# A graph network kernel: layer 1's two norms, residual and next product in one chunked pass, and a bias as a 65th row of weights

## The chip, the core and the metric

The kernel runs on one core of a Trainium2 chip. The core has a matrix engine (TensorE, PE in the profile; PEld are its weight loads), a vector engine (VectorE, DVE), an activation engine (ScalarE, ACT), GpSimd (POOL), which here mostly issues gathers and scatters by index, and SyncE (SP), which issues the other transfers. The metric is device microseconds of one launch, lower is better.

## What is computed

Four residual graph layers on 6250 nodes of 128 features and 106250 edges. Each is fed by `h = relu(layernorm(x))`. The stretch that is changed lies between the first layer's result and the third layer's first product:

```
h = relu(layernorm(x));  x = x + L0(h)            # two attention layers, then a dense product with Wlin, blin
h = relu(layernorm(x));  x = x + L1(h)            # L1: xw = h @ W; out = adjacency-weighted sum of xw, + b;
                                                  #     out = layernorm(out) * ln_gamma + ln_beta
h = relu(layernorm(x));  x = x + L2(h)            # L2 begins with h[src] @ W1.T + b1, taken here as (h @ W1.T + b1)[src]
```

## The kernel before, in words

The nodes lie as 49 blocks (`NB`) of 128 rows, one row to a partition, so a tensor of all nodes is 128 partitions x 6272 elements. `Xn` holds x, `B0`, `B1`, `B2` are buffers of that size, `accn` is another in `ACC`. Work "by chunk" takes four blocks (`CB`), so 13 chunks (`CHUNKS`), the last with one block. A stage ends with a barrier of all engines (`end`, `S.end_stage`). The stages around the change, in order:

- `into_layer_1` (L2126): a software pipeline by chunk, its order written out in `on_vector`, `on_scalar`, `on_tensor` (at step s, chunk s minus a fixed lag). DVE mixes (`mix`, L2174 and L2180), ACT takes exp and relu, DVE joins them (L2196), PE turns the chunk (`turn`, L2203), ACT copies it (L2210), PE multiplies it by Wlin (`multiply`, 64 rows of weights, L2218) and adds the bias with a second matmul of one row of ones (L2219), ACT takes exp and relu of the result (L2227, L2228), DVE adds it to x with row sums (`join_again`, L2236, L2241, L2244), ACT in `norm` makes relu(x - mean) (L2252) and the squares (L2256), PE turns it again (L2263) and multiplies by the layer's W (`multiply_again`, L2276), and DVE moves it to `B1` (`move`, L2282). After all chunks DVE takes roots, scales (L2286), SP stores the rows to `table` (L2292). Meanwhile POOL scatters edge weights into the dense adjacency (L1061); it began that before the stage and must be done before it ends.
- `mixed_pass` (L1075): PE sums the layer's messages as 1666 matmuls against the dense adjacency (L1190), loaded by SP, and 70 groups by gathered rows (L1180). DVE adds (L1135, L1142) and, at the end of each part, multiplies by `scale` and adds the bias (`finish`, L1148, L1149). ACT has nothing to do. `meanwhile` (L948) loads the bias row and would run steps given to it first; here there are none.
- then a stage written at the foot of `gnn` (L2485 to L2500), each operation over all 6272 elements and waiting for the one before (`go`): add `ln_beta` to x (L2488); `centre` (L632: row sums L635, subtract L637, square on ACT L638, row sums L639, `inv_sqrt` L644 to L654); times the root, times `ln_gamma`, add to x (L2490 to L2492); `centre` again; then `dense` (L671) in chunks of seven blocks: stage with relu (L664), turn (L715), copy on ACT (L722), multiply by W1 (L730), add bias (L739), store to `table` (L748). POOL clears `accn` (L2497) beside the second `centre`.
- `pair_pass` (L1553): POOL gathers rows of `table` (L977, four DMAs to a group), back to back over the whole pass.

Of the kernel before, what the change touches and what calls it, by code (L numbers as in the profile page):

```python
# [19 lines left out]
P = 128  # L20
# [6 lines left out]
GT = 4  # L27
# [102 lines left out]
def gnn(nc, A, out):  # L130
    S = Sems(nc)
    ve, ac, pe, po, sp = nc.vector, nc.scalar, nc.tensor, nc.gpsimd, nc.sync
    with ExitStack() as ctx:
# [115 lines left out]
        def tall(a, width=D):  # L249

            return a.unsqueeze(2).broadcast_to([P, a.shape[1], width])

        Xn, B0, B1, B2 = X[:, :, :], BUF[0][:, :, :], BUF[1][:, :, :], BUF[2][:, :, :]
# [821 lines left out]
        def mixed_pass(xw, scale, result, ring_at, beside):  # L1075
# [15 lines left out]
            added, after_add, after_dense = [0], {}, {}  # L1091
            ends = {c: max(n for n, unit in enumerate(units) if unit[0] == c) for c in range(DENSE)}

            with ExitStack() as ps:
# [50 lines left out]
                def finish(part):  # L1145
                    b, w = part
                    o = result[:, b:b + w, :]
                    write(lambda: ve.tensor_tensor(o, o, tall(scale[:, b:b + w]), ALU.mult))  # L1148
                    write(lambda: ve.tensor_tensor(o, o, wide(bias[:, :], w), ALU.add))  # L1149
# [46 lines left out]
                on_vector()  # L1196
                multiply()
# [928 lines left out]
        def into_layer_1(acc, c_e, c_s):  # L2126
# [29 lines left out]
            with ExitStack() as ps:  # L2156
# [5 lines left out]
                def loads():  # L2162
                    sp.dma_start(wmat[0:C2, :], A["L0_gnn_Wlin"]).then_inc(S("weights"), 16)
                    sp.dma_start(wbias[0:1, :], A["L0_gnn_blin"].rearrange("(a n) -> a n", a=1)).then_inc(S("weights"), 16)
                    sp.dma_start(wmat_l[:, :], A["L1_gnn_W"]).then_inc(S("weights"), 16)

# [45 lines left out]
                def multiply(c):  # L2212
# [3 lines left out]
                    for j in range(chunk(c)[0]):  # L2216
                        to = lin[c % 2][:, j * P:(j + 1) * P]
                        pe.matmul(to, XT[0:C2, c % 2, j * P:(j + 1) * P], wmat[0:C2, :], start=True, stop=False)  # L2218
                        m = pe.matmul(to, ones[0:1, :], wbias[0:1, :], start=False, stop=True)  # L2219
# [10 lines left out]
                def join_again(c):  # L2230
# [13 lines left out]
                    ve.tensor_scalar(less_mean[:, at], total[:, at], -1.0 / D, None, ALU.mult).then_inc(S("mean"), 1)  # L2244

                def norm(c):

                    ac.wait_ge(S("mean"), c + 1)
                    wait(ac, S("turned_again"), c - 1)
                    for j in range(chunk(c)[0]):  # L2250
                        b = c * CB + j
                        ac.activation(Z[c % 2][:, j * P:(j + 1) * P], Xn[:, b, :], ACT.Relu, bias=less_mean[:, b:b + 1]  # L2252
                                      ).then_inc(S("normed"), 1)
# [75 lines left out]
                def on_tensor():  # L2329
                    pe.wait_ge(S("weights"), 48)  # L2330
                    for s in range(CHUNKS + 6):
# [4 lines left out]
                loads()  # L2336
                degrees()
# [10 lines left out]
                keep_roots()  # L2348
                sp.wait_ge(S("stored"), 16 * CHUNKS)
# [135 lines left out]
        mixed_pass(accn, dinv_guarded[:, :], B0, BUF[1:], (A["L1_gnn_b"], D, []))  # L2485
        begin()
        load_all([(gain[:, :], spread(A["L1_gnn_ln_gamma"], D)), (bias[:, :], spread(A["L1_gnn_ln_beta"], D))])
        go(ve, lambda: ve.tensor_tensor(Xn, Xn, wide(bias[:, :]), ALU.add))  # L2488
        rstd = centre(B0, B0, B1)
        go(ve, lambda: ve.tensor_tensor(B0, B0, tall(rstd), ALU.mult))  # L2490
        go(ve, lambda: ve.tensor_tensor(B0, B0, wide(gain[:, :]), ALU.mult))
        go(ve, lambda: ve.tensor_tensor(Xn, Xn, B0, ALU.add))  # L2492

        po.wait_ge(chain[0].sem, chain[0].n)
        po.memset(accn, 0.0)  # L2497
        rstd = centre(Xn, B0, B1)
        dense(B0, A["L2_gnn_W1"], B1, D, D, A["L2_gnn_b1"], prepare=relu_times(rstd), store=table)

        end()
# [39 lines left out]
```

## Time and profile before

| what | value |
|---|---|
| median of 3 runs | 7088.94 us (7073.95 to 7094.61) |
| the profiled execution, its own time | 7090.57 us |
| its span | 7088.8 us |
| granted TensorE clock, mean | 0.856 of full |
| layer-1 stage (`into_layer_1`) | about 3767.5 to 3899.9 us of the span |
| `mixed_pass` | about 3899.9 to 4357.4 |
| norms, residual and product | about 4357.4 to 4472.7 |
| `pair_pass` | from 4472.7 |

The profile is of one execution. Its rows give the start on the engine in us from the span's start, the length, the engine, the line, the operation with what it writes and reads, how often in a row (x4), and in brackets how long the engine sat idle just before and what ended that. Where several instructions are in one row, the length runs from the first start to the last end. Granted clock 1.0 is 2.4 GHz, 0.5 is 1.2 GHz.

### The profile page before, as it was taken

Reading aid. Unit: us, or ns where it says so; the run is one execution under the profiler, and the core shown is the slowest. Engines: PE = TensorE matmul, PEld = TensorE weight load, DVE = VectorE, ACT = ScalarE, POOL = GpSimd, SP = SyncE. Lnnn points to the kernel's source line nnn. Section 1 sums busy time; section 2 is a strip of 40 time slices with the busy share of each in tenths; the row PEclk is TensorE's granted clock in tenths of the full one; section 3 lists DMA queues with packets and bytes.
Section 4 is the critical chain, followed back from the end, with each engine's and each line's share of the span. In section 5 each row is a group of like instructions: output and inputs, shape, how many; then the busy total and the mean of one; then the engine's idle time right before and its main releaser. Section 6 shows DMA issues by size and latency. Waiting matters only on the chain. (4 is left out here: it accounts for less than half of the span.)

```text
span 7088.8 us, 112592 instructions
## 1 busy us (share of the span) xinstructions
PE 5454.1 (77%) x30592; PEld 4368.9 (62%) x30592; DVE 3803.6 (54%) x12536; ACT 2082.9 (29%) x6605; POOL 4608.6 (65%) x4393
## 2 busy tenths in 40 slices
PE   1588888828776888885887995566666579999999
PEld 0477777716665777774775995566666445555555
DVE  5655553248985555422885345566666444444344
ACT  0133334328962333332996000222222310000000
POOL 1477777738877777777886671577777337377373
PEclk9877888759977888876996998788888799999999
DMA  4388886646743444334442883555555369999998
GB/s 171 115 270 266 269 260 176 130 92 140 144 83 85 105 105 105 90 80 55 76 76 35 301 289 134 151 157 159 158 157 159 63 212 307 305 298 304 298 307 264
DMA packets 902935, 1231.49 MB, mean 174 GB/s; under 512 B 230297, under 2 KB 639917, under 8 KB 889463
## 3 DMA queue, kind: packets, MB, share of 16 engines
q1 hardware_dynamic: 599528, 866.62, 38.5%
q0 software_dynamic: 207392, 219.55, 17.1%
q10 hardware_dynamic: 95372, 137.95, 5.6%
q8 instruction: 256, 4.19, 0.2%
q14 instruction: 387, 3.17, 0.1%
HBM read 987.45 MB, written 237.38 MB: 173 GB/s over the span
## 5 line engine op out<-in xcount | busy, mean ns | idle before, releaser
L977 POOL DMA_INDIRECT ACC<-table,TABS x1760 | 1716.7, 975 | 684.1 <-issue 648.2
L1282 POOL DMA_INDIRECT BUF<-table,TABS x840 | 796.5, 948 | 627.9 <-DMA table<-ACC 274.4
L1061 POOL DMA_INDIRECT adjacency<-TABS x600 | 960.3, 1601 | 258.3 <-issue 220.6
L977 POOL DMA_INDIRECT BUF<-table,TABS x880 | 835.1, 949 | 319.3 <-issue 319.3
L1735 PE MATMUL picked<-ident,ACC 128*128 128x128 f32 (+1 forms) x3520 | 868.0, 338 | 0.0
L1734 PE MATMUL picked<-G,OH 128*128 128x128 f32 (+1 forms) x2352 | 624.6, 358 | 300.1 <-DVE G L1713 200.3
L2056 PE MATMUL asum<-BUF 128*128 128x144 f32 x3520 | 561.3, 305 | 167.3 <-DVE BUF L2034 162.7
L1811 DVE SCALAR_TENSOR_TENSOR BUF<-BUF,TABS,wspread 128x128 bf16<-128x128 f32 (+1 forms) x600 | 324.5, 541 | 647.9 <-issue 638.5
L1734 PEld LDWEIGHTS picked<-G,OH 128*128 128x128 f32 (+1 forms) x2352 | 438.1, 222 | 375.7 <-DVE G L1713 279.2
L1735 PEld LDWEIGHTS picked<-ident,ACC 128*128 128x128 f32 (+1 forms) x3520 | 666.5, 220 | 0.0
L1645 PE MATMUL sums<-BUF,OH 128*128 128x128 f32 x1760 | 316.8, 337 | 393.7 <-DVE BUF L1631 393.7
L2056 PEld LDWEIGHTS asum<-BUF 128*128 128x128 f32 x3520 | 476.5, 197 | 198.1 <-issue 183.8
L2002 ACT ACTIVATE BUF<-iota_row,TABS 128x128 f32<-128x128 f32 x1760 | 555.2, 386 | 97.5 <-PEq L88 97.5
L1755 PEld LDWEIGHTS lcol<-attT,BUF 128*128 128x128 f32 (+1 forms) x3520 | 459.9, 202 | 145.6 <-issue 134.8
L1645 PEld LDWEIGHTS sums<-BUF,OH 128*128 128x128 f32 x1760 | 271.3, 236 | 433.7 <-issue 433.7
L1007 DVE TENSOR_TENSOR ACC<-ACC,asum 128x144 f32 (+1 forms) x1760 | 462.9, 263 | 96.3 <-PE asum L2056 15.5
L1755 PE MATMUL lcol<-attT,BUF 128*128 128x8 f32 (+1 forms) x3520 | 480.6, 259 | 2.7 <-ACT BUF L1773 2.7
L1761 ACT ACTIVATE ACC<-lcol 128x32 f32<-128x32 f32 (+1 forms) x440 | 81.5, 185 | 1305.0 <-PE lcol L1755 1293.7
L1747 DVE TENSOR_TENSOR BUF<-BUF,picked 128x512 f32<-128x512 f32 (+1 forms) x440 | 297.2, 676 | 237.3 <-ACT BUF L1741 237.3
L1713 DVE TENSOR_SCALAR G<-BUF,iota_col 128x512 f32<-128x512 bf16 x440 | 219.5, 499 | 352.5 <-DMA BUF<-locals 347.0
L1190 PE MATMUL sums<-ACC,BUF 128*128 128x128 f32 x3332 | 387.3, 277 | 23.2 <-DMA BUF<-adjacency 13.5
L1190 PEld LDWEIGHTS sums<-ACC,BUF 128*128 128x128 f32 x3332 | 380.6, 193 | 25.0 <-DMA BUF<-adjacency 13.9
(384 smaller groups left out, 10042.7 us busy)
## 6 DMA issues: line engine op xcount, KB each, us to landing
TABS<-adjacency SPq DMA_DIRECT2D x272, 512.0 KB
BUF<-in_edge_pair SPq DMA_DIRECT2D x880, 128.0 KB
BUF<-adjacency SPq DMA_DIRECT2D x102, 1024.0 KB
BUF<-adjacency SPq DMA_DIRECT2D x204, 512.0 KB, 5.1
adjacency<-zeros ACTq DMA_DIRECT2D x56, 1792.0 KB
G<-adjacency SPq DMA_DIRECT2D x136, 512.0 KB
kept<-ACC SPq DMA_DIRECT2D x220, 272.0 KB, 3.3
G<-kept SPq DMA_DIRECT2D x220, 272.0 KB
```

The costliest lines, as they stand in the source:

```text
L977: po.indirect_dma_start(rows[:, slot, j, 0:width], None, tab, bass.IndirectOffsetOnAxis(ap=SRC[:, q * GT + j:q * GT + j + 1], axis=0)).the ...
L1007: ve.tensor_tensor(at, at, self.from_[:, j, 0:self.width], ALU.add).then_inc(S("added"), 1)
L1061: po.indirect_dma_start(adj_flat, bass.IndirectOffsetOnAxis(ap=PLACE[:, k:k + 1], axis=0), TOTAL[:, k:k + 1], None, compute_op=ALU.add).th ...
L1190: m = pe.matmul(sums[:, j, 0:P], RA[n % len(RA)][:, (i * w + j) * P:(i * w + j + 1) * P], xw[:, b + i, :], start=b + i == 0, stop=b + i == ...
L1282: po.indirect_dma_start(R[:, q % deep_ring, j, :], None, table, bass.IndirectOffsetOnAxis(ap=SRC[:, k:k + 1], axis=0)).then_inc(S(f"gather ...
L1645: m = pe.matmul(sums[h][:, j, :], OH[:, h, j, :], V[:, q % 3, j, :], start=True, stop=True)
L1734: pe.matmul(z, XRB[q % 3][:, j, :], OHT[:, slot, j, :], start=True, stop=False)
L1735: m = pe.matmul(z, R[:, q % DEEP, j, :], ident[:, :], start=False, stop=True)
L1755: m = pe.matmul(lcol[slot % 2][:, j * H:(j + 1) * H], Z[:, q % 3, j * P:(j + 1) * P], attT[0:W, 0:H], start=True, stop=True)
L1811: ve.scalar_tensor_tensor(JUNK[:, at % 3, 0:j + 1, :], KEYS[:, n % 2, 0:j + 1, :], KEY[:, k:k + 1], wspread[:, 0:j + 1, :], ALU.is_equal, ...
L2002: ac.activation(HOT[:, slot, j, :], iota_row[:, :], ACT.Abs, scale=-1.0, bias=LOCAL[:, bass.ds(q * GT + j, 1)]).then_inc(S("gap"), 1)
L2056: m = pe.matmul(sums[slot % 2][:, j, 0:WIDE], HOT[:, slot, j, :], RHS[:, slot, j, :], start=True, stop=True)
```

## The change

In `into_layer_1`, `blin` is loaded into row 64 of `wmat` and a row of ones is written once into row 64 of `XT`; the product is then one matmul of 65 rows for each block, and the bias matmul goes. The relu(x - mean) of four blocks moves from ACT to DVE, behind the means. The rows `ln_gamma` and `ln_beta` are loaded here. In `mixed_pass`, adding `ln_beta` to x becomes a step of `meanwhile`, `finish` goes block by block and takes row sums along, and ACT squares the finished blocks. The stage of whole-tensor operations is replaced by `into_pair_pass`, a pipeline by chunk: DVE shifts and scales by gamma, adds to x with row sums, takes the mean and makes relu(x - mean); ACT squares, copies and moves; PE turns and multiplies; at the end DVE scales each block by its root, adds the bias, and SP stores.

```diff
                 def finish(part):
                     b, w = part
-                    o = result[:, b:b + w, :]
-                    write(lambda: ve.tensor_tensor(o, o, tall(scale[:, b:b + w]), ALU.mult))
-                    write(lambda: ve.tensor_tensor(o, o, wide(bias[:, :], w), ALU.add))
+                    for i in range(b, b + w):
+                        o = result[:, i, :]
+                        write(lambda: ve.scalar_tensor_tensor(o, o, scale[:, i:i + 1], bias[:, :], ALU.mult, ALU.add,
+                                                              accum_out=total[:, i:i + 1]))
+                    write(lambda: ve.tensor_scalar(less_mean[:, b:b + w], total[:, b:b + w], -1.0 / D, None, ALU.mult))
+                    finished.append((added[0], part))
...
+                def square():
...
+                    for n, (b, w) in finished:
+                        ac.wait_ge(S("added"), n)
+                        for i in range(b, b + w):
+                            wait(ac, S("squared"), done)
+                            ac.activation(unread, result[:, i, :], ACT.Square, bias=less_mean[:, i:i + 1],
+                                          accum_out=squares[:, i:i + 1]).then_inc(S("squared"), 1)
+                            done += 1
...
                     for j in range(chunk(c)[0]):
-                        to = lin[c % 2][:, j * P:(j + 1) * P]
-                        pe.matmul(to, XT[0:C2, c % 2, j * P:(j + 1) * P], wmat[0:C2, :], start=True, stop=False)
-                        m = pe.matmul(to, ones[0:1, :], wbias[0:1, :], start=False, stop=True)
+                        m = pe.matmul(lin[c % 2][:, j * P:(j + 1) * P], XT[0:C2 + 1, c % 2, j * P:(j + 1) * P], wmat[0:C2 + 1, :],
+                                      start=True, stop=True)
...
                     ve.tensor_scalar(less_mean[:, at], total[:, at], -1.0 / D, None, ALU.mult).then_inc(S("mean"), 1)
+                    ve.wait_ge(S("mean"), c + 1)
+                    wait(ve, S("turned_again"), c - 1)
+                    for j in range(blocks):
+                        b = c * CB + j
+                        ve.tensor_scalar(Z[c % 2][:, j * P:(j + 1) * P], Xn[:, b, :], less_mean[:, b:b + 1], 0.0, ALU.add, ALU.max
+                                         ).then_inc(S("normed"), 1)
...
                     ac.wait_ge(S("mean"), c + 1)
-                    wait(ac, S("turned_again"), c - 1)
-                    for j in range(chunk(c)[0]):
-                        b = c * CB + j
-                        ac.activation(Z[c % 2][:, j * P:(j + 1) * P], Xn[:, b, :], ACT.Relu, bias=less_mean[:, b:b + 1]
-                                      ).then_inc(S("normed"), 1)
...
                 loads()
+                ve.memset(XT[C2:C2 + 1, :, :], 1.0).then_inc(S("one_row"), 1)
                 degrees()
...
+        def into_pair_pass():
...
+                def add(c):
...
+                    for b in range(at.start, at.stop):
...
+                        ve.scalar_tensor_tensor(y, B0[:, b, :], less_mean[:, b:b + 1], gamma, ALU.add, ALU.mult
+                                                ).then_inc(S("shifted"), 1)
+                    for b in range(at.start, at.stop):
...
+                        ve.wait_ge(S("shifted"), b + 1)
+                        ve.scalar_tensor_tensor(Xn[:, b, :], y, squares[:, b:b + 1], Xn[:, b, :], ALU.mult, ALU.add,
+                                                accum_out=total[:, b:b + 1]).then_inc(S("summed"), 1)
+                    ve.wait_ge(S("summed"), up_to(c))
+                    ve.tensor_scalar(mean_2[:, at], total[:, at], -1.0 / D, None, ALU.mult).then_inc(S("mean"), 1)
+                    ve.wait_ge(S("mean"), c + 1)
+                    wait(ve, S("turned"), c - 1)
+                    for b in range(at.start, at.stop):
...
+                        ve.tensor_scalar(z, Xn[:, b, :], mean_2[:, b:b + 1], 0.0, ALU.add, ALU.max).then_inc(S("normed"), 1)
...
+                def scale(c):
...
+                    ve.wait_ge(S("moved"), c + 1)
+                    for b in range(at.start, at.stop):
+                        m = ve.scalar_tensor_tensor(B1[:, b, :], B1[:, b, :], var_2[:, b:b + 1], wbias[:, :], ALU.mult, ALU.add)
+                    m.then_inc(S("scaled"), 1)
...
+                def on_scalar():
+                    for s in range(CHUNKS + 2):
+                        for piece, late in ((square, 0), (copy, 1), (move, 2)):
...
+                def on_tensor():
+                    pe.wait_ge(S("weights"), 32)
+                    for s in range(CHUNKS + 2):
+                        for piece, late in ((turn, 0), (multiply, 1)):
...
+                po.memset(accn, 0.0).then_inc(S("cleared"), 1)
...
+                for c in range(CHUNKS):
+                    add(c)
+                on_scalar()
+                on_tensor()
+                ve.wait_ge(S("squared"), NB)
...
+                for c in range(CHUNKS):
+                    scale(c)
+                    store(c)
```

On TensorE, in the layer-1 stage, one steady step reads in a row like this before (`out` is the second product, `tp` and `tq` are the two turnings, `lin` the product with Wlin):

```order
L2276 MATMUL out_53<-wmat_l,G 128x128 x4
L2203 MATMUL tp_48<-ident,BUF 64x128 x4
L2263 MATMUL tq_51<-ident,BUF 128x128 x4
L2218 MATMUL lin_49<-wmat,OH 128x128
L2219 MATMUL lin_49<-wbias,ones 128x128
L2218 MATMUL lin_49<-wmat,OH 128x128
L2219 MATMUL lin_49<-wbias,ones 128x128
L2218 MATMUL lin_49<-wmat,OH 128x128
L2219 MATMUL lin_49<-wbias,ones 128x128
L2218 MATMUL lin_49<-wmat,OH 128x128
L2219 MATMUL lin_49<-wbias,ones 128x128
L2276 MATMUL out_54<-wmat_l,G 128x128 x4
```

and on the same engine and place now:

```order
L2299 MATMUL out_53<-wmat_l,G 128x128 x4
L2226 MATMUL tp_48<-ident,BUF 64x128 x4
L2286 MATMUL tq_51<-ident,BUF 128x128 x4
L2240 MATMUL lin_49<-wmat,OH 128x128 x4
L2299 MATMUL out_54<-wmat_l,G 128x128 x4
```

The four bias matmuls between the products are gone; the rest keeps its order.

On VectorE, in the same stage, one steady step before:

```order
L2236 SCALAR_TENSOR_TENSOR BUF<-BUF 128x512
L2241 SCALAR_TENSOR_TENSOR X,gain<-BUF,X 128x128 x4
L2244 TENSOR_SCALAR gain<-gain 128x4
L2282 COPY BUF<-out_54 128x512
L2174 SCALAR_TENSOR_TENSOR BUF<-ACC,st,bias 128x64 x4
```

and now:

```order
L2258 SCALAR_TENSOR_TENSOR BUF<-BUF 128x512
L2263 SCALAR_TENSOR_TENSOR X,gain<-BUF,X 128x128 x4
L2266 TENSOR_SCALAR gain<-gain 128x4
L2271 TENSOR_SCALAR BUF<-X,gain 128x128 x4
L2305 COPY BUF<-out_54 128x512
L2197 SCALAR_TENSOR_TENSOR BUF<-ACC,st,bias 128x64 x4
```

Four operations of one block each (L2271) came in ahead of the move.

On VectorE, from the end of `mixed_pass` on, before (whole-tensor operations):

```order
L1149 TENSOR_TENSOR BUF<-BUF,bias 128x256
L2488 TENSOR_TENSOR X<-X,bias 128x6272
L635 TENSOR_REDUCE st<-BUF 128x49
L636 TENSOR_SCALAR st<-st 128x49
L637 TENSOR_TENSOR BUF<-BUF,st 128x6272
L639 TENSOR_REDUCE st<-BUF 128x49
L640 TENSOR_SCALAR st<-st 128x49
L649 RECIPROCAL st<-st 128x49
```

and now (finish of the last part, roots, then the first chunks of `into_pair_pass`):

```order
L1152 SCALAR_TENSOR_TENSOR BUF,st<-BUF,dinv_guarded,bias 128x128 x2
L1154 TENSOR_SCALAR gain<-st 128x2
L2494 TENSOR_SCALAR gain<-gain 128x49
L650 RECIPROCAL st<-gain 128x49
...
L2416 SCALAR_TENSOR_TENSOR BUF<-BUF,gain,att 128x128 x4
L2421 SCALAR_TENSOR_TENSOR X,st<-BUF,gain,X 128x128 x4
L2424 TENSOR_SCALAR st<-st 128x4
L2429 TENSOR_SCALAR BUF<-X,st 128x128 x4
L2416 SCALAR_TENSOR_TENSOR BUF<-BUF,gain,att 128x128 x4
```

Ten passes over the whole tensor (L2488, L635, L637, L639, L2490 to L2492, and `centre` again) became twelve short operations and one tiny one to each full chunk.

## Rows read from the trace of the kernel before

**Rows 1.** The page's granted TensorE clock in 40 slices, tenths.

```profile
PEclk9877888759977888876996998788888799999999
```

**Rows 2.** Busy by stage: window, us, PE, PEld, DVE, ACT, POOL, PEclk, DMA, GB/s.

```profile
3767.50:3899.90 132.40, 100.55 (x394) 75.83 (x394) 68.38 (x287) 68.59 (x229) 76.10 (x48) 0.59 0.24 26
3899.90:4357.40 457.50, 439.58 (x3892) 438.10 (x3892) 180.23 (x597) 0.00 (x0) 268.81 (x280) 0.99 0.80 280
4357.40:4470.00 112.60, 19.80 (x147) 18.82 (x147) 85.18 (x38) 17.77 (x11) 5.33 (x1) 0.59 0.11 31
```

**Rows 3.** Timeline of PE in the layer-1 stage: start, us, engine, line, operation.

```profile
3779.09 0.79 PE L2218 MATMUL lin<-wmat,OH 64*128 64x128 f32 x2
...
3780.53 0.79 PE L2218 MATMUL lin<-wmat,OH 64*128 64x128 f32 x2
...
3817.01 2.07 PE L2276 MATMUL out<-wmat_l,G 128*128 128x128 f32 x8
3818.88 1.06 PE L2203 MATMUL tp<-ident,BUF 128*64 128x128 f32 x4
...
3820.61 0.49 PE L2218 MATMUL lin<-wmat,OH 64*128 64x128 f32 x2
...
3821.44 0.49 PE L2218 MATMUL lin<-wmat,OH 64*128 64x128 f32 x2
...
3823.95 2.07 PE L2276 MATMUL out<-wmat_l,G 128*128 128x128 f32 x8
...
3871.26 0.79 PE L2218 MATMUL lin<-wmat,OH 64*128 64x128 f32 x2
```

**Rows 4.** Timeline of DVE in the same stage, one step.

```profile
3825.17 0.69 DVE L2236 SCALAR_TENSOR_TENSOR BUF<-BUF 128x512 f32<-128x512 f32 x1 [2.55 <-ACT BUF L2228]
...
3826.33 0.29 DVE L2241 SCALAR_TENSOR_TENSOR X<-BUF,X 128x128 f32<-128x128 f32 x1
...
3826.54 0.29 DVE L2241 SCALAR_TENSOR_TENSOR X<-BUF,X 128x128 f32<-128x128 f32 x1
...
3826.87 0.17 DVE L2244 TENSOR_SCALAR gain<-gain 128x4 f32<-128x4 f32 x1
...
3829.15 0.41 DVE L2196 SCALAR_TENSOR_TENSOR BUF<-BUF 128x256 f32<-128x256 f32 x1
```

**Rows 5.** Timeline of ACT in the same step.

```profile
3827.35 0.39 ACT L2256 ACTIVATE BUF<-X,gain 128x128 f32<-128x128 f32 x1
...
3827.73 0.58 ACT L2270 ACTIVATE G<-tq 128x512 f32<-128x512 f32 x1
```

**Rows 6.** Timeline, end of that stage: scaling on DVE, stores on SP's queue.

```profile
3884.82 7.52 DVE L2286 TENSOR_TENSOR ACC<-BUF,st 128x512 f32<-128x512 f32 x13
3885.59 10.54 SPq L2292 DMA_DIRECT2D table<-ACC  x13
```

**Rows 7.** Timeline of POOL: last scatter, a slow gather, first gather of `pair_pass`.

```profile
3857.74 1.57 POOL L1061 DMA_INDIRECT adjacency<-TABS  x1 [0.30 <-issue]
...
3905.55 4.44 POOL L1112 DMA_INDIRECT G<-table,TABS  x1 [0.30 <-issue]
...
4472.75 0.95 POOL L977 DMA_INDIRECT BUF<-table,TABS  x1 [51.26 <-issue]
```

**Rows 8.** Timeline of DVE in `mixed_pass`: its first add, two of the last.

```profile
3932.61 1.15 DVE L1135 TENSOR_TENSOR BUF<-BUF,near 128x128 f32 x3 [21.63 <-PE near L1180]
...
4333.02 0.69 DVE L1142 TENSOR_TENSOR BUF<-BUF,sums 128x512 f32<-128x512 f32 x1 [11.70 <-PE sums L1190]
...
4356.02 0.42 DVE L1142 TENSOR_TENSOR BUF<-BUF,sums 128x256 f32<-128x256 f32 x1 [20.86 <-PE sums L1190]
```

**Rows 9.** Timeline of DVE between `mixed_pass` and `pair_pass`: first and last operation.

```profile
4361.43 6.69 DVE L2488 TENSOR_TENSOR X<-X,bias 128x6272 f32<-128x6272 f32 x1 [4.07 <-DMA bias<-in_L_gnn_ln_beta]
...
4466.36 1.09 DVE L739 TENSOR_TENSOR BUF<-yp,wbias 128x896 f32<-128x896 f32 x1 [0.47 <-PE yp L730]
```

**Rows 10.** Groups of instructions by line: one-block TENSOR_SCALAR; count, busy us, mean ns.

```profile
L989 DVE TENSOR_SCALAR OH<-iota_row,TABS 128x128 f32<-128x128 f32 x880 | 192.2, 294 | 0.0
```

More of the change, by code:

```diff
@@ L251, in tall @@
             return a.unsqueeze(2).broadcast_to([P, a.shape[1], width])
+        less_mean, squares = gain[:, 0:NB], gain[:, NB:2 * NB]
         Xn, B0, B1, B2 = X[:, :, :], BUF[0][:, :, :], BUF[1][:, :, :], BUF[2][:, :, :]
@@ L1091, in mixed_pass @@
             added, after_add, after_dense = [0], {}, {}
+            finished, total = [], st[0][:, 0:NB]
             ends = {c: max(n for n, unit in enumerate(units) if unit[0] == c) for c in range(DENSE)}
@@ L1146, in finish @@
                     b, w = part
-                    o = result[:, b:b + w, :]
-                    write(lambda: ve.tensor_tensor(o, o, tall(scale[:, b:b + w]), ALU.mult))
-                    write(lambda: ve.tensor_tensor(o, o, wide(bias[:, :], w), ALU.add))
+                    for i in range(b, b + w):
[5 more added lines that the diff above has]
+                def square():
+                    unread = G[:, :, :, :].rearrange("p r t d -> p (r t d)")[:, RING * GT * D:RING * GT * D + D]
+                    done = 0
+                    for n, (b, w) in finished:
[5 more added lines that the diff above has]
+                            done += 1
+                    assert done == NB
+                    ac.wait_ge(S("squared"), NB)
                 def on_vector():
@@ L1196, in mixed_pass @@
                 on_vector()
+                square()
                 multiply()
@@ L2163, in loads @@
                     sp.dma_start(wmat[0:C2, :], A["L0_gnn_Wlin"]).then_inc(S("weights"), 16)
-                    sp.dma_start(wbias[0:1, :], A["L0_gnn_blin"].rearrange("(a n) -> a n", a=1)).then_inc(S("weights"), 16)
+                    sp.dma_start(wmat[C2:C2 + 1, :], A["L0_gnn_blin"].rearrange("(a n) -> a n", a=1)).then_inc(S("weights"), 16)
                     sp.dma_start(wmat_l[:, :], A["L1_gnn_W"]).then_inc(S("weights"), 16)
+                    sp.dma_start(att[:, :], spread(A["L1_gnn_ln_gamma"], D)).then_inc(S("for_layer_1"), 16)
+                    sp.dma_start(wbias_l[:, :], spread(A["L1_gnn_ln_beta"], D)).then_inc(S("for_layer_1"), 16)
                 def mix(c):
@@ L2330, in on_tensor @@
                     pe.wait_ge(S("weights"), 48)
+                    pe.wait_ge(S("one_row"), 1)
                     for s in range(CHUNKS + 6):
@@ L2484, in gnn @@
         into_layer_1(acc, c_e, c_s)
[L2485 to L2501, printed above, removed]
+        mixed_pass(accn, dinv_guarded[:, :], B0, BUF[1:],
+                   (A["L1_gnn_b"], D, [lambda: ve.tensor_tensor(Xn, Xn, wide(wbias_l[:, :]), ALU.add)]))
+        into_pair_pass()
         pair_pass(accn)
```

74 lines of the change are left out of this document (added).

## The prediction, made before the changed kernel ran

> **What bounds the kernel now.** I read the stage windows first. In `mixed_pass` PE is busy 439.6 of 457.5 us, so nothing DVE or ACT do there counts while they keep up. In the next 112.6 us no engine is full: DVE has 85.2, PE 19.8, ACT 17.8, one after the other. In the layer-1 stage PE has 100.6 of 132.4 us and no other engine 77 [rows 2]. Then the timelines. In the layer-1 stage the second product starts at 3817.01 and again at 3823.95, a step of 6.94 us, and PE has no gap in it: out 1.87, two turnings 1.73, the product with Wlin four times 0.83 (3820.61 to 3821.44 for one block with its bias) [rows 3]. Earlier, at the low clock (1.2 GHz), one such block takes 1.44 (3779.09 to 3780.53). From product 0 (3779.09) to product 12 (3871.26) twelve steps take 92.2 us, 7.7 each [rows 3]. DVE waits in each step for ACT, which waited for PE [rows 4]. Last, `pair_pass`: its gathers on POOL start at 4472.75 [rows 7] and run back to back, so it begins when the stage before ends and hands every us on.
>
> **Layer-1 stage.** The bias matmuls go, and with them the change of shape between every two matmuls (64 rows, 1 row). The nearest row for four blocks of one-shape products is out, 1.87 at the low clock [rows 3]. PE's step is then at most 1.87 + about 2.0 for the turnings + 1.87 = 5.7, less where the clock rises. DVE's step was 4.4 us (L2236 at 3825.17 to L2196's end at 3829.56). It gains four relus. One-block operations follow one another every 0.21 (3826.33 to 3826.54) though each is 0.29 long [rows 4]; the one-source kind is 0.294 long [rows 10]. So 0.84, and 0.1 for the wait on the means: 5.3 (0.6 for the four would be the low end, 1.2, at full length each, the high one). ACT loses four activations and has slack. The new wait on `turned_again` has DVE's move and mixes queued behind it, but it asks for a turning two chunks back, done a step earlier. I take 5.5 us a step for the eight full steps and 4 for the four in which the pipeline fills, 60 in all against 92.2: minus 32. The memset of the row of ones stands at the head of DVE and costs about 0.9 (between 0.5 and 1.5). The end of the stage then comes while POOL's last scatters are in flight (they end at 3859.3 [rows 7]); the stores, 10.5 us for 13 [rows 6], may be slowed by 1. **Minus 30.** The two rows for gamma and beta are transfers nobody waits for before the barrier.
>
> **mixed_pass.** Adding beta to x costs DVE 6.7 us [rows 9], ahead of its first operations. It is covered: DVE sits idle 21.6 us before its first add [rows 8]. Without cover it would cost its 6.7. The finishing of 43 blocks was 15.7 us of DVE and becomes some 20 (each operation waits for the one before: 0.4 each); DVE then still waits, having had 11.7 us of idleness before the next sum [rows 8]. The squares on ACT have an engine without work [rows 2]. Only the last part shows: after the add at 4356.02 came 0.9 us of finishing; now two block operations at 0.4, one of 0.2, and two squares on ACT at 0.6 with handovers, 2.5 in all.
>
> **The new stage**, from the add at 4356.02 to the first gather at 4472.75 [rows 7, 8], 116.7 us before. After:
> - add 0.45 and finish 2.5;
> - barrier 2.0 (the 4.07 before L2488 held it and a bias load [rows 9], so 1.5 to 4);
> - roots of the first variance, seven tiny operations of 0.17 and up [rows 4] and one on ACT, 2.0;
> - 12.25 chunks. DVE: eight two-source operations at 0.21, four relus at 0.21, a mean and two waits 0.45, 2.95 a chunk. ACT: four squares at 0.38 (3827.35 to 3827.73), a copy and a move at 0.5 [rows 5], 2.5. PE: turning 1.0 and product 1.87 [rows 3], 2.9 at the low clock. Three engines within reach of each other, so I take 3.0: 36.8;
> - from the last relu to the last move, the pipeline's run-out (square, turning, copy, product, move): 4.0;
> - roots again, 1.5;
> - 49 scalings at 0.21, 10.4, with the stores running along. The same 3.2 MB took SP 10.5 us to issue [rows 6], so the stores end with or 1 to 2 us behind the scaling;
> - last store to first gather, 5.3, as before (L739 ends at 4467.45 [rows 9]).
>
> Sum 64.9, **minus 51.8**. Clearing `accn` (5.3 us of POOL [rows 2]) has the whole stage as cover.
>
> A rule of the Trainium skill speaks against this part: "VectorE: DVE Perf Modes", section "The TRN2 errata — SBUF-src ops pay a fixed extra latency per instruction", says that short operations pay a fixed cost each and advises tiles of 512 elements or more. The rows agree in kind: 6272 elements in one operation are 6.7 us [rows 9], 49 operations at 0.21 are 10.3. That is in the sum already. What the change saves is passes and waits between them.
>
> **The sum.** 7090.6 (the profiled execution's own time) minus 30 minus 51.8 is 7008.8. The median of the runs is 1.6 lower, so 7007; I say **7008**.
>
> **Rivals.**
> *The short operations do not overlap.* Where each waits, they may run at full length 0.29 plus a handover instead of every 0.21. For: DVE's three adds of `mixed_pass` take 1.15 [rows 8], about 0.43 from one to the next, where each waits for its forerunner. Against: in the new stage the producers lie four operations back, as in L2241. Price: 12 operations at 0.29 make a chunk 4.0 (plus 12), the scalings 14.2 (plus 4), the layer-1 relus plus 4: 7029.
> *The one-shape product stays slow.* If 64 or 65 rows cost what they do now (0.72 a block at the low clock, half of 1.44 [rows 3]), PE's step is 1.87 + 2.0 + 2.9 = 6.8 at the low clock, above DVE: 1.3 over 12 steps, 7024. The Trainium skill, "TensorEngine Tiling (Array Packing)", section "Key Properties", says that a change of tiling mode drains the engine. By that rule the whole excess goes with the mode changes; the trace has only the mixed sequence, and its low-clock block, 1.44 for four records, against 0.47 for the two of out [rows 3], fits it.
> *Two-port operations hold POOL.* A gather next to DVE's memset took 4.44 us instead of 0.95 [rows 7]. If the 49 new relus held up the scatters by 0.5 each, POOL would end at 3884 instead of 3859.3, the stage closing about 14 us later than I have it: 7022. Against: a relu is 0.2 to 0.3 long, and the scatters have some 10 us of slack. The Trainium skill, "SBUF — State Buffer", section "SBUF: two separate sides", describes such an exclusive lock.
> *Slower than before.* The last two passes run at a granted clock of 0.9 and more [rows 1]. Were the 112 us of near idleness what lets the chip grant that, their loss would lower it. The last ten slices are 1770 us bound by PE; a clock lower by 4.7% there costs 83 us and cancels the gain, and at 6% the time is 7115. Against: `mixed_pass` has 0.99 right behind a stage of 0.59, and holds it for 457 us [rows 2].
> That the code does not do what it says is no rival: the order of instructions shows the passes and the bias matmuls gone.
>
> **How the numbers follow.** The forecast gets 0.76 (its own range 6998 to 7019: 0.2 us more or less a chunk in two stages and the barrier's bounds), the short operations 0.10, the slow product 0.07, POOL 0.04, slower 0.02, and 0.01 lies elsewhere. The range 6994 to 7032 takes in the first four and leaves out less than 2 in 10. A measurement of this kernel can tell 0.3%, 21 us. All but the last two cases are faster by more: faster 0.97, same 0.01, slower 0.02.
>
> **What would show it.** Product 0 to product 12 in the layer-1 stage about 60 us apart; `lin` at 0.23 or less a record; out to out 5.5 us. DVE's starts in `into_pair_pass` 0.21 apart, its chunks 3.0 apart, scalings 10 to 11 us in all, and the first gather of `pair_pass` about 65 us after the last add of `mixed_pass`. `mixed_pass` itself and all passes behind unchanged within 1 to 2 us. I am wrong if a chunk in either stage waits in a ring from engine to engine, if POOL is the last at the layer-1 barrier, or if the granted clock behind the stage changes.

## The result

The median of four runs is 7011.35 us (6998.27 to 7016.03), that of the kernel before, run beside it, 7085.13 (7073.95 to 7094.61). The ratio is 0.9894, with a 95% interval of 0.9873 to 0.9914. A second chip, where the kernel before took 8530.84 us (11 runs), gave 8443.9 (6 runs), a ratio of 0.9898 (0.9873 to 0.9923). Forecast: 7008.

In the profiled execution (own time 7016.03, span 7014.2) the windows that answer to [rows 2] are, with the same columns:

```profile
3765.00:3858.50 93.50, 48.51 (x296) 43.58 (x296) 76.72 (x321) 54.29 (x178) 73.19 (x46) 0.70 0.32 36
3858.50:4316.00 457.50, 439.00 (x3892) 437.71 (x3892) 188.06 (x677) 23.24 (x94) 275.44 (x280) 0.99 0.80 280
4316.00:4389.00 73.00, 25.09 (x149) 19.23 (x148) 61.69 (x276) 33.53 (x130) 6.26 (x2) 0.75 0.17 46
```

The first and third window were 132.4 and 112.6 us long. PE lost half of its busy time in the first (100.6 to 48.5), and DVE is now the fullest engine of both. `mixed_pass` between them is as it was. The granted clock of the whole, to be held against [rows 1]:

```profile
PEclk9877888859977888876998999787888799999999
```

Cut at the same instructions, the two executions differ as follows:

| stretch | before | after | difference |
|---|---|---|---|
| span's start to DVE's first operation of the layer-1 stage | 3771.17 | 3762.85 | -8.3 |
| layer-1 stage, to SP's issue of the bias load behind its barrier | 127.95 | 95.71 | -32.2 |
| from there to the last add of `mixed_pass` | 456.90 | 457.67 | +0.8 |
| last add to the first gather of `pair_pass` | 116.73 | 71.84 | -44.9 |
| first gather to the span's end | 2616.0 | 2626.1 | +10.1 |

The two changed stretches give 77.1, `mixed_pass` takes 0.8 back. The first and the last row hold code that the change does not touch; they nearly cancel here, and are looked at below.

**The layer-1 stage.** PE with two full chunks, one at the low clock and one at the high (columns as in [rows 3]):

```profile
3784.91 1.06 PE L2286 MATMUL tq<-ident,BUF 128*128 128x128 f32 x4
3785.76 1.92 PE L2240 MATMUL lin<-wmat,OH 65*128 65x128 f32 x8
3787.47 1.91 PE L2299 MATMUL out<-wmat_l,G 128*128 128x128 f32 x8
3789.17 0.72 PE L2226 MATMUL tp<-ident,BUF 128*64 128x128 f32 x4
3789.73 0.60 PE L2286 MATMUL tq<-ident,BUF 128*128 128x128 f32 x4
3790.16 1.06 PE L2240 MATMUL lin<-wmat,OH 65*128 65x128 f32 x8
3791.06 1.06 PE L2299 MATMUL out<-wmat_l,G 128*128 128x128 f32 x8
```

The product with 65 rows of weights starts 1.71 us ahead of the one with 128 rows at the low clock and 0.90 ahead at the high one, as long as that one itself: 0.21 and 0.11 for each of its eight records. Four blocks had cost four times 1.44 or 0.83 [rows 3]. One step of DVE:

```profile
3799.55 0.68 DVE L2258 SCALAR_TENSOR_TENSOR BUF<-BUF 128x512 f32<-128x512 f32 x1
...
3801.27 0.47 DVE L2266 TENSOR_SCALAR gain<-gain 128x4 f32<-128x4 f32 x1
3801.77 0.88 DVE L2271 TENSOR_SCALAR BUF<-X,gain 128x128 f32<-128x128 f32 x4
3802.56 0.69 DVE L2305 COPY BUF<-out 128x512 f32<-128x512 f32 x1
...
3805.13 0.68 DVE L2258 SCALAR_TENSOR_TENSOR BUF<-BUF 128x512 f32<-128x512 f32 x1
```

A step is 5.58 us with nothing in brackets, so DVE waits for nobody: it was idle 2.55 us a step [rows 4]. The four moved relus take 0.8. The window and, below it, the end of the stage on SP and POOL:

```profile
3785.00:3820.00 35.00, 25.11 (x159) 23.77 (x158) 34.31 (x158) 27.91 (x93) 29.21 (x20) 0.79 0.22 1
```

```profile
3839.88 11.26 SPq L2315 DMA_DIRECT2D table<-ACC  x13
3850.33 1.57 POOL L1062 DMA_INDIRECT adjacency<-TABS  x1 [0.30 <-issue]
3851.19 0.34 SPq L224 DMA_DIRECT2D dinv_rows<-OH  x1
3858.56 0.34 SPq L953 DMA_DIRECT2D bias<-in_L_gnn_b  x1
```

DVE is busy 34.3 of 35.0 us. At the end SP is through at 3851.53, yet its next issue comes 7.03 us later. In the kernel before that was 2.24:

```profile
3896.19 0.69 SPq L224 DMA_DIRECT2D dinv_rows<-OH  x1
3899.12 0.35 SPq L952 DMA_DIRECT2D bias<-in_L_gnn_b  x1
```

What came last is POOL's last scatter (3850.33 plus 1.57, then its landing). POOL has become the last at this barrier, for 4.8 us.

**The new stage**, DVE and POOL at its head and its end:

```profile
4316.23 0.42 DVE L1144 TENSOR_TENSOR BUF<-BUF,sums 128x256 f32<-128x256 f32 x1 [20.52 <-PE sums L1210]
...
4319.39 5.32 POOL L2493 MEMSET ACC<- 128x6272 f32 x1 [69.93 <-POOLq L88]
4319.43 5.33 DVE L2494 TENSOR_SCALAR gain<-gain 128x49 f32<-128x49 f32 x1 [1.79 <-PEq L88]
...
4326.52 1.14 DVE L2416 SCALAR_TENSOR_TENSOR BUF<-BUF,gain,att 128x128 f32<-128x128 f32 x4
4327.58 0.35 DVE L2421 SCALAR_TENSOR_TENSOR X<-BUF,gain,X 128x128 f32<-128x128 f32 x1
...
4327.85 0.35 DVE L2421 SCALAR_TENSOR_TENSOR X<-BUF,gain,X 128x128 f32<-128x128 f32 x1
...
4366.53 0.29 DVE L2429 TENSOR_SCALAR BUF<-X,st 128x128 f32<-128x128 f32 x1
...
4371.39 12.95 DVE L2470 SCALAR_TENSOR_TENSOR BUF<-BUF,st,wbias 128x128 f32<-128x128 f32 x49
4372.61 12.50 SPq L2477 DMA_DIRECT2D table<-BUF  x13
4388.07 0.95 POOL L978 DMA_INDIRECT BUF<-table,TABS  x1 [63.35 <-issue]
```

The second row from the top of these is POOL clearing `accn`. Beside it, the first tiny operation of the roots, 49 elements a partition, takes 5.33 us. And each operation with two tensors and a scalar per block is 0.35 long and 0.27 behind its forerunner, where the prediction had 0.21. In the chunks DVE has nearly no gap:

```profile
4326.50:4366.50 40.00, 22.25 (x128) 17.01 (x128) 39.06 (x208) 28.98 (x116) 0.00 (x0) 0.84 0.00 0
```

### The profile page after: what moved, and what is told of

It reads as the page before. It is cut to its first block and busy times, and to the rows that moved or that the text cites. A ratio compares the mean times of both kernels' runs of the same rounds, so it can differ in the third digit from the quotient of the medians.

```text
span 7014.2 us, 112904 instructions
## 1 busy us (share of the span) xinstructions
PE 5405.4 (77%) x30494; PEld 4331.6 (62%) x30494; DVE 3798.0 (54%) x12904; ACT 2107.7 (30%) x6769; POOL 4618.2 (66%) x4393
## 5 line engine op out<-in xcount | busy, mean ns | idle before, releaser
L1062 POOL DMA_INDIRECT adjacency<-TABS x600 | 962.6, 1604 | 253.9 <-issue 219.1
```

The source lines that it names most:

```text
L1062: po.indirect_dma_start(adj_flat, bass.IndirectOffsetOnAxis(ap=PLACE[:, k:k + 1], axis=0), TOTAL[:, k:k + 1], None, compute_op=ALU.add).th ...
```

## The experiments

Four things were open: the 5.33 us, the price of a block operation, what sets the length of the layer-1 stage, and whether the stretches with unchanged code belong to the change. "After" is the changed kernel. The runs marked "other chip" were made on two slower chips, at a granted clock of 0.79: the kernel before and the three single parts where the kernel before takes 8509 us, the shared relus, the four edits and after again where it takes 8531. Whole times are compared only on one chip.

**Clearing `accn` later.** After, with one move:

```diff
-                po.memset(accn, 0.0).then_inc(S("cleared"), 1)
                 go(ve, lambda: ve.tensor_scalar(squares...
...
+                po.wait_ge(S("scaled"), 1)
+                po.memset(accn, 0.0).then_inc(S("cleared"), 1)
                 po.wait_ge(S("cleared"), 1)
```

> The changed kernel, but GpSimd clears accn only after the first chunk of the last scaling (beside two-source operations), not at the start of the new stage. Theory (the 5.33 us of the tiny L2494 is the time for which the memset holds a port pair that this one-source operation needs): L2494 goes to 0.2 us, the first chunk starts 5.1 us earlier, the new stage (last add of mixed_pass to first gather of pair_pass) goes from 71.8 to 66.7 us. Rival (the first operation behind a barrier is slow whatever GpSimd does): L2494 stays at 5.3 and the stage at 71.8.

The timeline of this kernel, DVE's first root operation, the scalings and POOL:

```profile
4322.15 0.19 DVE L2493 TENSOR_SCALAR gain<-gain 128x49 f32<-128x49 f32 x1 [1.79 <-PEq L88]
...
4368.96 12.95 DVE L2470 SCALAR_TENSOR_TENSOR BUF<-BUF,st,wbias 128x128 f32<-128x128 f32 x49
4370.16 5.33 POOL L2509 MEMSET ACC<- 128x6272 f32 x1 [117.96 <-DVE BUF L2470]
4385.66 0.95 POOL L978 DMA_INDIRECT BUF<-table,TABS  x1 [10.17 <-issue]
```

The same operation takes 0.19. The last add, at 4318.95, is 66.7 us before the gather instead of 71.8. The memset now runs beside the scalings, which stay at 12.95. So it was the memset; it held this operation of one source, and it does not hold those with two tensors and a scalar. One run took 7014.48 us: 5 us in a whole of 7011 is below what it can tell.

**The scalar of each block.** In the scalings a constant takes the place of the root of each block, so the rows' scale is left out of the result:

```diff
-ve.scalar_tensor_tensor(B1[:, b, :], B1[:, b, :], var_2[:, b:b + 1], wbias[:, :], ALU.mult, ALU.add)
+ve.scalar_tensor_tensor(B1[:, b, :], B1[:, b, :], 0.5, wbias[:, :], ALU.mult, ALU.add)
```

> The changed kernel with a constant 0.5 in place of the per-partition root in the 49 last scalings; the multiplication by the root is left out, all else stands. Theory (a per-partition scalar beside two tensors costs a block operation 0.05 us): the 49 scalings take 10.4 to 10.6 us instead of 12.95, 0.21 apart instead of 0.264. Rival (it is the third stream, the bias tile or the place in memory): 12.95 as before.

```profile
4361.35 9.99 DVE L2470 SCALAR_TENSOR_TENSOR BUF<-BUF,wbias 128x128 f32<-128x128 f32 x49
4362.34 10.58 SPq L2477 DMA_DIRECT2D table<-BUF  x13
```

49 operations in 9.99, 0.204 each (10.4 to 10.6 in all was expected), where the scalar read from memory made them 0.264. The 2.96 us do not all arrive: the stage took 70.2 instead of 71.8, since SP's 10.58 us of issues now end 1.6 us behind the scalings, where it was 0.8, and the gather follows them 0.5 us later than it did.

**Fewer scatters in the layer-1 stage.** A table says in which stage POOL issues the adjacency's groups of four scatters. Four groups move one stage ahead:

```diff
-MERGES = ((4, 2, 58, 12), (4, 4, 54, 12))
+MERGES = ((4, 2, 58, 12), (4, 4, 58, 8))
```

> The changed kernel with 4 of the 12 scatter groups that run beside the layer-1 stage issued one stage earlier (16 scatters, 30 us of GpSimd). Theory (GpSimd, done at 3851.9 and then waiting for its scatters to land, is the last at that stage's barrier): the layer-1 stage (memset of the row of ones to the issue of the bias load of mixed_pass) goes from 95.7 to about 92 us, since the barrier follows the landing of dinv by 1 us and not by 4.9. Rival (the barrier's 4.9 us is something else): 95.7. The stage that takes the scatters may get longer by up to 30 us; that says only where they fit.

```profile
3839.45 1.57 POOL L1062 DMA_INDIRECT adjacency<-TABS  x1 [0.30 <-issue]
...
3870.61 0.66 SPq L224 DMA_DIRECT2D dinv_rows<-OH  x1
3873.52 0.34 SPq L953 DMA_DIRECT2D bias<-in_L_gnn_b  x1
```

POOL is done 30 us before SP, and SP goes on 2.25 us after its last store, as in the kernel before. The stage took 90.3 us instead of 95.7 (92 was expected). So POOL's lateness was worth 5. But the stage starts 20 us later (3783.2 against 3762.85; four kernels with the same code up to there lie within 13 us of each other), and the whole took 7032.42 in one run: the stage ahead has no room for 16 more scatters.

**One part at a time.** The kernel before with both layer-1 edits alone (the row of ones and the relus on DVE), then with each, then with neither but everything else; and the kernel before itself, on the chip of the last three.

> The kernel before with the layer-1 stage's part of the change alone (bias as 65th row, relu by DVE). If the parts add up, product 0 to product 12 takes 56 to 57 us as in the changed kernel (92.2 before), and the stage is 32 us shorter; the whole time about 7057. Rival (part of the gain hangs on the other parts, over the granted clock): less than 28 us.

> The kernel before, unchanged, for a second profile. The stretch from the first gather of the last three passes to the end took 1332.5 us in the first profile of before, and 1338.8 to 1342.9 in five profiles of kernels with parts of the change. Theory (this is scatter from run to run of a stretch that DMA and PE share, nothing of the change): a value above 1337 here. Rival (something in the change makes the last passes 8 us longer): 1332 to 1334 again.

> The kernel before with the bias as 65th row alone; the relus stay on ACT. PE's step falls to 5.7 at most, DVE's stays 4.4, ACT's is 5.35 (6.93 less 1.58 of idleness). Theory (removing the bias matmuls carries the whole gain of the layer-1 stage): product 0 to product 12 in 56 to 60 us. Rival (both parts are needed): 70 or more.

> The kernel before with the four relus moved to DVE alone; the bias matmuls stay. Theory (PE is the bound there, so this moves nothing): product 0 to product 12 in 88 to 93 us (92.2 before). Rival (ACT's part of the ring counted): 80 or less.

> The changed kernel with the layer-1 stage's part undone: bias matmuls back, relus back on ACT. Theory (the parts add up): product 0 to product 12 92 us, last add of mixed_pass to first gather of pair_pass 71.8 as in the changed kernel, the whole about 7043. With GpSimd done early again in the layer-1 stage its barrier follows the landing of dinv by about 1 us. Rival (the clock or the transfers tie the stages): the second stretch differs by more than 2 us from 71.8.

| kernel | first layer-1 mix to first gather of `mixed_pass` | last add to first gather of `pair_pass` | last gathered passes, to the end | time |
|---|---|---|---|---|
| before | 127.4 | 116.7 | 1332.5 | 7090.57 |
| after | 94.1 | 71.8 | 1341.1 | 7016.03 |
| layer-1 edits only | 94.3 | 116.5 | 1338.8 | 7057.25 |
| before, other chip | 129.9 | 116.6 | 1545.8 | 8508.66 |
| row of ones only, other chip | 95.0 | 117.1 | 1538.4 | 8464.34 |
| relus only, other chip | 122.5 | 117.4 | 1551.2 | 8514.5 |
| all but the layer-1 edits, other chip | 132.3 | 71.8 | 1547.4 | 8467.26 |
| after, other chip | 94.3 | 71.9 | 1553.3 | 8443.9 |

(The last time is a median of six, the others are single executions; those scatter by more than the relus' 7 us, which the whole times do not show.) The two parts add up: each appears in its own column with its full size and leaves the other alone. Inside the layer-1 stage they do not add up. The row of ones brings 34.9 us by itself, the relus 7.4, both together 35.6 (33 on the faster chips). The windows tell why. Relus only, row of ones only:

```profile
4605.00:4640.00 35.00, 35.00 (x136) 26.97 (x134) 21.55 (x99) 16.72 (x56) 29.21 (x20) 0.59 0.22 1
```

```profile
4600.00:4620.00 20.00, 14.55 (x92) 12.44 (x92) 13.92 (x66) 20.00 (x70) 16.65 (x12) 0.84 0.21 1
```

With the bias matmuls left in, PE is busy 35.0 of 35.0 us, and taking work from ACT brings 4.1 between products 0 and 12 (90.6 instead of 94.7) and 3.3 from product 12 to the first store. The kernel before had PE wait 2.7 us for ACT's relus in 27 us early in the stage; with the relus on DVE there is no such wait. With the bias matmuls gone and the relus left on ACT, ACT is busy 20.0 of 20.0; its step, from the first to the next of its relu groups (4602.45 and 4607.67), is 5.2 us. That is shorter than the 5.6 of DVE in the kernel after: in the steady steps the relus' move exchanges a full ACT for a full DVE. Over the whole stage the move does bring something, since the last steps are shorter with it: products 0 to 12 take 60.1 us with the row alone and 56.0 with both (other chip), and SP is through with its last issue 90.9 us after the first mix and 86.3. The end of the stage does not show it. Row of ones only:

```profile
4643.23 2.12 POOL L1061 DMA_INDIRECT adjacency<-TABS  x1 [0.30 <-issue]
4648.59 0.64 SPq L224 DMA_DIRECT2D dinv_rows<-OH  x1
4652.56 0.35 SPq L952 DMA_DIRECT2D bias<-in_L_gnn_b  x1
```

POOL's last scatter ends 87.0 us after the first mix (4558.36), as in all kernels that issue the same scatters (86.2 to 87.3). With the row alone SP waits 3.33 us at the barrier, 1 more than where POOL is early; with both edits it waits 7, and that takes most of the 4.6 us of the relus' move back (95.0 and 94.3 in the table).

**Half of the relus back to ACT** (other chip). After, with blocks 0 and 1 of a step on DVE, 2 and 3 on ACT:

```diff
-                    for j in range(blocks):
+                    for j in range(min(2, blocks)):
...
+                    for j in range(2, chunk(c)[0]):
+                        ac.activation(Z[c % 2][:, j * P:(j + 1) * P], Xn[:, b, :], ACT.Relu, bias=less_mean[:, b:b + 1]...
```

> The kernel after with the four relus of a layer-1 step shared out: blocks 0 and 1 by VectorE, 2 and 3 by ScalarE, nothing else. Theory (VectorE is the bound of the step, busy 34.3 of 35.0 us in 3785:3820 at 5.59 us a step): a step loses about 0.5 us, to 5.0 to 5.2, because two relus of 0.20 each leave VectorE while ScalarE (27.9 of 35.0 busy) takes two of 0.26; the first product to the thirteenth takes 51 to 54 us instead of 56.6. Rival (the step is a chain of hand-overs, and no engine's work): it stays at 5.5 to 5.7 and the stage is unchanged. By both, the barrier behind the stage still waits for GpSimd's last scatters, so that of the some 4 us at most 1 to 2 reach the first near gather: whole kernel within 0.1% of the kernel after, by the theory 7008 to 7014 where that takes 7011.

```profile
4629.23 0.29 DVE L2263 SCALAR_TENSOR_TENSOR X<-BUF,X 128x128 f32<-128x128 f32 x1
...
4634.03 0.29 DVE L2263 SCALAR_TENSOR_TENSOR X<-BUF,X 128x128 f32<-128x128 f32 x1
...
4638.96 0.29 DVE L2263 SCALAR_TENSOR_TENSOR X<-BUF,X 128x128 f32<-128x128 f32 x1
```

A step is 4.8 to 4.9 us, less than was expected: DVE was indeed the bound. The products then take 54.5 us instead of 56.0, just outside the 51 to 54 expected, since in some of the twelve steps the pipeline fills or drains. And the stage from the first mix to the first gather takes 94.2, against 94.3, though SP is through after 85.0 us. Three kernels with steps of 5.2, 5.6 and 4.9 us all end at 94 to 95. That is POOL: it issues its 48 scatters at its own pace beside them, and the first gather comes 7 to 8 us behind the last.

**Four edits together**: the memset behind the roots, the shared relus, one of four relus of the new stage on ACT, and one group of scatters a stage earlier (55, 11). The kernel after was timed beside it, both on the other chip.

> The kernel after with four edits together: the memset of accn goes behind the roots (5.1 us measured for it alone), the layer-1 relus are shared between VectorE and ScalarE (two blocks each), one of four relus of the new stage is ScalarE's, and one scatter group of the second half is merged one stage earlier (4, 4, 55, 11 instead of 4, 4, 54, 12). Theory: the stretch from the last mixed add to the first pair gather takes 63 to 65 us instead of 71.8 (5.1 for the memset, 12 chunks times 0.15 to 0.2 for the relus); the layer-1 stage with its barrier takes 91 to 94 instead of 95.7, since GpSimd's last scatter comes 2 us earlier; together 9 to 12 us, a ratio to the kernel after of 0.9983 to 0.9987, 6999 to 7002 where that takes 7011. Rival (the stage ahead is already full of scatters and pays for the group that is moved there, as 58 and 8 paid some 20 us): the first layer-1 mix starts 4 us or more later, and the sum is 3 to 8 us.

> The kernel after, unchanged, timed beside the kernel with the four edits on the same chip, so that the two can be compared through the kernel before. Both theories: a ratio to the kernel before of 0.988 to 0.991. If the 8 to 10 us by which the last three passes were longer in the profiled execution of after belong to the change (rival), they are there again, 1341 us and more from their first gather to the end, while the kernel before's are 1332; if they are scatter between executions (theory), the stretch differs from the former 1341.1 by up to 5 us either way.

| | this kernel | after |
|---|---|---|
| first layer-1 mix to first gather | 87.5 | 94.3 |
| last add to first gather of `pair_pass` | 64.9 | 71.9 |
| median of six, lowest to highest | 8453.9 (8426 to 8463) | 8443.9 (8438 to 8457) |
| ratio to before (95%) | 0.9906 (0.9879 to 0.9933) | 0.9898 (0.9873 to 0.9923) |

Both stretches are 7 us shorter, the second as the theory had it, the first by more than its 2 to 5, and the medians show none of the 14 (the two profiled executions alone would have: 8432.7 and 8453.74). So the kernel was timed once more, where the kernel before took 7101 us:

> The kernel with the four edits once more, since its six runs (8426 to 8463 us) and the six of the kernel after (8438 to 8457) lay across each other although the two stages were 7.0 us shorter each in its profile. Theory (the 14 us are real, and the scatter of the executions hides them): a ratio to the kernel before of 0.986 to 0.989, where after had 0.9894 and 0.9898, with both stages again 65 and 87 us. Rival (what the two stages save is lost elsewhere, in the scatter stage that took one more group, or in the last passes): the ratio is 0.989 to 0.991 again, and the first layer-1 mix or the last passes lie some 10 us later than the kernel before's order of the run would have them.

7022.55 us (six runs) against 7101.15 for the kernel before (eleven), a ratio of 0.9895 (0.9877 to 0.9913); after had 0.9894. The stretches were 88.0 and 64.8 us again.

The ratio came out as the rival had it, but the intervals are 0.18% to either side, 13 us, about the size of the gain sought. Its first layer-1 mix stood at 3772.7, 7.5 us later than in after, and its last passes took 1342.3. The moved group may have cost part of the 7.5, since four groups cost 20. But on the chip where both ran, its first mix came only 1.8 us behind that of after (4585.5 and 4583.7), and that of the kernel with the shared relus alone, which has the same code up to there as after, at 4595.5. Three edits without the move were not run. It is not shown that this kernel beats after.

## Why the prediction was right

**The total** was forecast 7008 and measured 7011.35. The sum of steps for the profiled execution was 7008.8, its own time 7016.03. The two changed stretches were predicted at 81.8 together and gave 77.1. That the median lies 3 us from the forecast is in part luck: the four executions spread over 18 us, one stage gave 2.2 us more and the other 6.9 less than forecast, and the unchanged stretches moved by -8.3 and +10.1.

**What bounded the kernel**: right. The layer-1 stage was PE's at the low clock, the third window one engine after another. Both shrank, and all that they lost reached `pair_pass`. `mixed_pass` did not move (+0.8): adding beta, 6.69 us on DVE, and the finer finishing lie in DVE's idleness as said.

**Layer-1 stage**: 30 predicted, 32.2 measured. Products 0 to 12 lie 56.6 us apart (3771.64 to 3828.22) where 60 was forecast, with a step of 5.58 against 5.5: fewer of the twelve are full steps. The memset of the row is 0.91 (0.9 forecast), the stores 11.26 instead of 10.54 (1 forecast). From product 12 to the first store it takes 11.7 instead of 14.3, which was not in the sum. Against these stand the 4.8 us of POOL at the barrier. The prediction named that as a way to be wrong, with scatters held up by relus as its cause; the scatters were not held up, the stage closed earlier beside an unchanged POOL. The slack was there in the row of the last scatter [rows 7]: 3857.74 and 1.57 more, 40 us before the old barrier, and the stage was to lose 30 to 32 and the landing to be added.

**The relus' price** was right (0.84 forecast, 0.79 to 0.88 measured), but that their move brings next to nothing (95.0 us with the row alone, 94.3 with both) was not seen. The step without them was not worked out: ACT at 5.2 against DVE at 5.5. What it still brings, 4.6 us at SP's last issue, goes for the most part to the wait for POOL. The second of these edits was counted within a sum that the first earns alone.

**The new stage**: 51.8 predicted, 44.9 measured. Term by term:

| term | forecast | measured | from |
|---|---|---|---|
| add, finish, barrier | 4.95 | 3.20 | 4316.23 to 4319.43 |
| first roots | 2.0 | 7.09 | to 4326.52 |
| chunks | 36.8 | 40.30 | to 4366.82 |
| run-out and second roots | 5.5 | 4.57 | to 4371.39 |
| scalings | 10.4 | 12.95 | to 4384.34 |
| to the gather | 5.3 | 3.73 | to 4388.07 |
| sum | 64.95 | 71.84 | |

Two steps failed. The first is the sentence that clearing `accn` "has the whole stage as cover". It has, but in time only: POOL's memset shuts out such a DVE operation of one source for its whole length, and the first thing behind the barrier is one. The prediction weighed this for relus against scatters and for a gather next to DVE's memset [rows 7], and did not put the question to POOL's memset. Undone, the 5.1 us came back. The Trainium skill, "SBUF — State Buffer", section "SBUF: two separate sides", has the exclusive lock; the trace agrees for the one-source operation (5.33 beside the memset, 0.19 without). The same passage lets an operation with two inputs in SBUF collide only with a GpSimd operation that reads SBUF; the scalings, 12.95 beside the memset and without, agree with that.

The second is the term "eight two-source operations at 0.21". That row (L2241, [rows 4]) has a constant as its scalar. Those of the new stage read one from memory, which makes 0.27. Over 12.25 chunks and 49 scalings this is 8 times 0.06 times 12.25, 5.9, and 2.9; the mean and its two waits, 0.32 instead of 0.45, and the relus, 0.79 instead of 0.84, took 2.2 of the first back. The trace of before had a fitting row, of 128x128 elements with a scalar for each partition and two tensors (its result is bf16), in the groups by line:

```profile
L1811 DVE SCALAR_TENSOR_TENSOR BUF<-BUF,TABS,wspread 128x128 bf16<-128x128 f32 x150 | 52.1, 347 | 647.9 <-issue 638.5 <-PE wspread L1794 9.4
```

347 ns against the 289 of L2241. That three engines are within reach of each other in these chunks was wrong with it: DVE had 39.06 of 40.0 us, PE 22.25, since PE's clock was 0.84.

**The rivals.** Short operations that do not overlap (7029): they do, 0.27 apart at a length of 0.35. The one-shape product that stays slow (7024): no, 0.21 and 0.11 a record, so the old price belonged to the pair of a 64-row and a one-row product. Whether it was the change of shape or one of the two shapes by itself, no run tells. POOL held up by the relus (7022): a scatter takes 1604 ns in the mean (1601 before), though a relu's neighbour does wait now and then (L2266 took 0.47 instead of 0.17). Slower by the granted clock (7115): the last ten slices read the same in both pages, mean 0.863 against 0.856.

**Unchanged code** was said to stay within 1 to 2 us, for the passes behind. It did not in the one pair of executions: 8.3 less ahead of the layer-1 stage, 10.1 more behind the new one, 8.6 of that in the last passes. There PE is busy for 1305.1 us before and 1306.2 after, and the clock is 0.99 in both. It waits more. The waits of PE in that stretch, before and after (total, times, longest):

```profile
PE ahead L1341 <- ACT OH L1509: 11.8, 8, 2.8
PE turned L1320 <- DMA BUF<-table,TABS: 6.9, 5, 2.2
```

```profile
PE ahead L1362 <- ACT OH L1530: 16.3, 12, 3.1
PE turned L1341 <- DMA BUF<-table,TABS: 9.9, 2, 5.1
```

On the faster chips all changed kernels, that with the layer-1 edits alone too, have 1338.8 to 1342.9 there, the single execution of before 1332.5. The two runs that were to settle it, before and after once more, fell on the slower chips, where neither expected value can be read off: the one of before has 1545.8 and the changed ones 1538.4 to 1553.3, the kernel after the highest. The first mix wanders as well: 3754.9, 3762.4, 3765.2, 3768.0 and, before, 3772.6, with the same code up to it but for a memset of 0.91. Scatter is the likelier reading, but a cost of a few us in the last passes is not excluded.

## What to carry to other kernels

When a pipeline is to replace whole-tensor operations, price each short operation by a row with the same kind of scalar, not only the same shape, and ask of every piece of work "beside" it whether the two engines shut each other out, even for a tiny first operation. When two edits remove work from one stage, work out the stage with each alone: the second may only hand the bound from one full engine to another, or run into a third that neither edit touches. And a stage that shrinks by 30 us needs the slack of every engine that merely had to be done by its end.

## What the runs showed of the hardware

- GpSimd's memset of 128x6272 f32 (5.32 us) held VectorE's one-source operation of 128x49 for 5.33 us instead of 0.19; 49 operations with two tensors and a scalar took 12.95 us beside the same memset and without it.
- It works the other way too: beside VectorE's addition of two tensors in memory, 6.69 us, and the copy of 1.15 us right behind it, a gather of GpSimd took 7.63 us instead of 0.95, so an operation with two tensors does hold GpSimd's gathers. The next gather, 5.13 us, fell beside VectorE's memset of 3.69 us, as one of 4.44 us did in the kernel before [rows 7]:

```profile
3862.91 6.69 DVE L2647 TENSOR_TENSOR X<-X,wbias_l 128x6272 f32<-128x6272 f32 x1 [15.04 <-DMA bias<-in_L_gnn_b]
3863.16 7.63 POOL L1114 DMA_INDIRECT G<-table,TABS  x1 [0.30 <-issue]
3871.09 5.13 POOL L1114 DMA_INDIRECT G<-table,TABS  x1 [0.30 <-issue]
3871.64 3.69 DVE L1173 MEMSET BUF<- 128x4352 f32 x1 [0.97 <-DVE BUF L1172]
```

- A scalar for each partition, read from memory, makes a 128x128 operation with two tensors 0.264 us from start to start, a constant 0.204.
- A product with 65 rows of weights runs at the pace of one with 128 (0.21 us a record at the low clock), a 64-row product alternating with a one-row product at 0.36.
- The granted clock of the layer-1 stage is 0.59 in the kernel before, with PE busy 76% of it, and 0.70 in the kernel after, with 52%; in the kernel after it changes level from one step to the next (3785.76 at 1.2 GHz and 3790.16 at 2.4 above).
